# Gathering graph rows on one Trainium2 core: fifteen or twenty-three chunks fetched row by row, by one queue or by two

## What is computed

```
xn   = layernorm(x)
agg  = segment_sum(xn[src], dst)            # 106250 edges, sorted by dst
h    = relu(agg @ W_rel + b_rel + xn @ W_root)
c    = sigmoid(i) * tanh(g);  y = (sigmoid(o) * tanh(c)) @ W_fc + b_fc     # i, g, o = h @ W_ih.T + b
x2   = x + y
w    = softmax over slices of layernorm(x2) @ W_x @ W_slice ...
out  = x2 + attention over slice tokens, spread back by w
```

## Time and profile before

| | us |
|---|---|
| median of 3 runs | 1237.53 (1236.96 to 1239.23) |
| profiled execution | 1240.34 |
| its span of instructions | 1238.5 |
| TensorE busy in the span | 1116.1 |
| ScalarE busy | 627.2 |
| GpSimd busy | 805.3 |

### The profile page before, as it was taken

The page is one execution under the profiler, slowest core; times in us unless marked ns, Lnnn a source line. Parts: engine busy times, 40 slices in busy tenths (PEclk is TensorE's granted clock), DMA queues, the critical chain, the costliest instruction groups (busy, mean ns, idle before and its releaser), DMA issues. The chain is left out here.

```text
span 1238.5 us, 30254 instructions
## 1 busy us (share of the span) xinstructions
PE 1116.1 (90%) x9821; PEld 967.1 (78%) x9821; DVE 831.8 (67%) x2560; ACT 627.2 (51%) x1257; POOL 805.3 (65%) x856
## 2 busy tenths in 40 slices
PE   1077799999999999999999999999999999999998
PEld 0046688878888888788888787888888878897798
DVE  7885476667666766676677756775767566746665
ACT  5872444554456454545554545455545454555332
POOL 5877777777777777777777777777777777400000
PEclk9998999999999999999999999999999999999999
DMA  8674444444454445444544444444444454313498
GB/s 313 225 268 119 125 130 136 147 142 136 129 148 142 141 124 150 140 140 123 150 149 138 121 148 150 137 121 150 147 136 122 150 149 137 97 44 116 129 336 290
DMA packets 92966, 188.74 MB, mean 152 GB/s; under 512 B 20914, under 2 KB 55591, under 8 KB 92821
## 3 DMA queue, kind: packets, MB, share of 16 engines
q0 software_dynamic: 39168, 107.01, 30.0%
q1 hardware_dynamic: 42794, 59.89, 14.8%
q10 hardware_dynamic: 10859, 20.05, 4.5%
HBM read 154.87 MB, written 32.00 MB: 151 GB/s over the span
## 5 line engine op out<-in xcount | busy, mean ns | idle before, releaser
L700 POOL DMA_INDIRECT ring<-table,sidx x798 | 763.5, 957 | 247.5 <-issue 242.7
L419 PE MATMUL ps<-h_h,wih_h 128*128 128x250 f32 x1200 | 338.8, 282 | 0.0
L420 PE MATMUL ps<-h_l,wih_h 128*128 128x250 f32 x1200 | 336.5, 280 | 0.0
L421 PE MATMUL ps<-h_h,wih_l 128*128 128x250 f32 x1200 | 336.5, 280 | 0.0
L419 PEld LDWEIGHTS ps<-h_h,wih_h 128*128 128x128 f32 x1200 | 230.1, 192 | 2.0 <-issue 0.8
L420 PEld LDWEIGHTS ps<-h_l,wih_h 128*128 128x128 f32 x1200 | 230.2, 192 | 1.1
L421 PEld LDWEIGHTS ps<-h_h,wih_l 128*128 128x128 f32 x1200 | 230.1, 192 | 0.0
L850 ACT ACTIVATE gate<-ps,bgate 128x250 f32<-128x250 f32 x300 | 124.2, 467 | 140.7 <-PE ps L421 139.7
L651 DVE TENSOR_SCALAR oneh<-iota,didx 128x64 f16<-128x64 f16 (+2 forms) x1179 | 183.1, 259 | 0.0
L1078 PE MATMUL ps<-ring,oneh 128*32 128x512 f16 x2280 | 151.0, 391 | 34.5 <-DMA ring<-table,sidx 31.9
L1078 PEld LDWEIGHTS ps<-ring,oneh 128*32 128x32 f16 x2280 | 59.5, 97 | 107.7 <-DMA ring<-table,sidx 46.4
(11 more groups left out here) (213 smaller groups left out, 2508.4 us busy)
## 6 DMA issues: line engine op xcount, KB each, us to landing
sp_ring<-table SPq DMA_DIRECT2D x1920, 1.0 KB
ring<-table,sidx POOLq DMA_INDIRECT x798
swt_d<-swt ACTq DMA_DIRECT2D x25, 500.0 KB
gate<-swt_d SPq DMA_DIRECT2D x19, 500.0 KB, 5.9
x_room<-in_x SPq DMA_DIRECT2D x12, 512.0 KB, 10.6
xn<-table SPq DMA_DIRECT2D x25, 224.0 KB
xin<-in_x SPq DMA_DIRECT2D x25, 224.0 KB
res<-xin SPq DMA_DIRECT2D x25, 224.0 KB
```

Of the source, the lines that this page charges most:

```text
L419: eng.matmul(dst, wh, xh, start=first, stop=False)
L420: eng.matmul(dst, wh, xl, start=False, stop=False)
L421: return eng.matmul(dst, wl, xh, start=False, stop=last)
L700: pool.indirect_dma_start(ring[:, j, :], None, table, bass.IndirectOffsetOnAxis(ap=idx, axis=0)).then_inc(done, 16)
```

## The change

Twenty-three chunks in place of fifteen are fetched row by row: chunk 86 and every 33rd after it, so about one in each turn. Of each chunk's 128 rows, SyncE fetches the first 88 and ScalarE the last 40, both into the same ring of three chunks and with the same semaphore. SyncE fetches 8, 16 and 64 rows in its turn's three places, and 88 in turn 0; it loads 22 addresses at a time. ScalarE fetches 20 rows in turn 0 and then rows at eleven places in its turn; it loads addresses 10 at a time at four of these. Both wait for room in the ring at a chunk's first row (`wait_slot`). ScalarE's turns are written out one by one, without a loop. The helpers for the slot, the addresses and one row are moved out of SyncE's block so that both can use them.

```diff
-    SP_FIRST, SP_STEP, SP_N, SP_SLOTS = 86, 52, 15, 3
+    SP_FIRST, SP_STEP, SP_N, SP_SLOTS = 86, 33, 23, 3
-    ROWS_FIRST, ROWS, LOADS = 96, (8, 16, 60), 32
+    ROWS_FIRST, ROWS, LOADS = 88, (8, 16, 64), 22
+    SP_ROWS = 4 * LOADS
+    ACT_ROWS = P - SP_ROWS
+    ACT_FIRST, ACT_LOADS = 20, 10
+        def wait_slot(eng, k):
+            if k == 0:
+                eng.wait_ge(spi_done, 1)
+            if k >= SP_SLOTS:
+                b = last_reader(SP_CHUNKS[k - SP_SLOTS])
+                eng.wait_ge(sum_done[b % 2], b // 2 + 1)
+                eng.wait_ge(sum_done[(b - 1) % 2], (b - 1) // 2 + 1)
+        def fetch_row(eng, k, q, start):
+            to = sp_ring[q:q + 1, k % SP_SLOTS, :].bitcast(U8)
+            eng.dma_start(to, rows8[ds(start, row_bytes)].rearrange("(p c) -> p c", p=1)).then_inc(
+                sp_rows[k % SP_SLOTS], 16)
...
+            def load_rows():
+
+                r = loaded[0]
+                if r < last_row and r < row_at[0] + ACT_LOADS:
+                    k, q = r // ACT_ROWS, r % ACT_ROWS
+                    if q == 0:
+                        wait_slot(act, k)
+                    for i, start in enumerate(load_starts(act, k, SP_ROWS + q, ACT_LOADS)):
+                        starts[r + i] = start
+                    loaded[0] += ACT_LOADS
+            def fetch_rows(n):
+
+                for r in range(row_at[0], min(row_at[0] + n, loaded[0])):
+                    fetch_row(act, r // ACT_ROWS, SP_ROWS + r % ACT_ROWS, starts.pop(r))
+                    row_at[0] += 1
...
                 if gnn:
                     split_x(t - 1)
+                    load_rows()
+                    fetch_rows(9)
                     relu_h(t - 1, 0)
...
-                    gates(t - 1, 0, 4)
+                    fetch_rows(2)
+                    gates(t - 1, 0, 2)
+                    load_rows()
+                    fetch_rows(1)
+                    gates(t - 1, 2, 4)
                     tanh_c(t - 1, 0)
+                    load_rows()
+                    fetch_rows(9)
...
-                    gates(t - 1, 4, 8)
+                    gates(t - 1, 4, 6)
+                    fetch_rows(1)
+                    gates(t - 1, 6, 8)
                     tanh_c(t - 1, 1)
+                    fetch_rows(4)
                     gates(t - 1, 8, 10)
+                    load_rows()
+                    fetch_rows(3)
...
                     gates(t - 1, 10, 12)
+                    fetch_rows(1)
                     high_hl(t - 1, 0)
+                    fetch_rows(1)
                     tanh_c(t - 1, 3)
...
                 if gnn:
+                    fetch_rows(1)
                     high_hl(t - 1, 1)
...
                     act.dma_start(swt_d[ds(p, 1)].rearrange("a p n -> p (a n)"),
                                   swt[:, :, :, :].rearrange("p e j n -> p (e j n)")).then_inc(swt_st, 16)
+                    fetch_rows(9)
...
-            with act.Fori(lo, hi, step) as t:
+            for t in range(lo, hi, step):
                 two_turns(turn, t)
```

More of the change, by code:

```diff
@@ L438, in out_count, with load_starts @@
             return 16 * (len(range(q, NCH + 1, TILES)) + (len(REST_PARTS) - 1 if q == NCH % TILES else 0))
+        rows8 = table.bitcast(U8).rearrange("n c -> (n c)")
+        row_bytes = 4 * C
+        def wait_slot(eng, k):
[5 more added lines that the diff above has]
+                eng.wait_ge(sum_done[(b - 1) % 2], (b - 1) // 2 + 1)
+        def load_starts(eng, k, q, n):
+            _, at = nc.values_load_multi_w_load_instructions(
+                sp_idx[k:k + 1, q:q + n], engines=[eng.engine], min_val=0, max_val=(N - 1) * row_bytes,
+                skip_runtime_bounds_check_because="the DMA checks its bounds")
+            return at
+        def fetch_row(eng, k, q, start):
+            to = sp_ring[q:q + 1, k % SP_SLOTS, :].bitcast(U8)
+            eng.dma_start(to, rows8[ds(start, row_bytes)].rearrange("(p c) -> p c", p=1)).then_inc(
+                sp_rows[k % SP_SLOTS], 16)
         @block.sync
@@ L517, in _ @@
             row_at = [0]
-            rows8 = table.bitcast(U8).rearrange("n c -> (n c)")
-            row_bytes = 4 * C
             def fetch_rows(n):
-                for r in range(row_at[0], min(row_at[0] + n, SP_N * P)):
-                    k, q = r // P, r % P
+                for r in range(row_at[0], min(row_at[0] + n, SP_N * SP_ROWS)):
+                    k, q = r // SP_ROWS, r % SP_ROWS
                     if q == 0:
[L526 to L531, removed]
-                    if q % LOADS == 0:
[L533 to L539, removed]
+                        wait_slot(sp, k)
+                    if q % LOADS == 0:
+                        starts[:] = load_starts(sp, k, q, LOADS)
+                    fetch_row(sp, k, q, starts[q % LOADS])
                 row_at[0] += n
@@ L548, in turn @@
                     for j, k in SP_OF.items():
-                        assert first_reader(j) // 2 > t or row_at[0] >= (k + 1) * P, (t, j, k, row_at)
+                        assert first_reader(j) // 2 > t or row_at[0] >= (k + 1) * SP_ROWS, (t, j, k, row_at)
                 if gather:
@@ L579, in _ @@
             last_turns(turn)
-            assert row_at[0] >= SP_N * P
+            assert row_at[0] >= SP_N * SP_ROWS
             def f_load(n, k):
@@ L873, in copy_out @@
                                ACT.Copy).then_inc(att_a, 1)
-            def turn(t, odd, gather, gnn, ffn, ahead):
+            row_at, loaded, starts = [0], [0], {}
+            last_row = SP_N * ACT_ROWS
+            def load_rows():
[11 more added lines that the diff above has]
+                    row_at[0] += 1
+            def turn(t, odd, gather, gnn, ffn, ahead):
+                if gather and t < NP - 1:
+                    for j, k in SP_OF.items():
+                        assert first_reader(j) // 2 > t or row_at[0] >= (k + 1) * ACT_ROWS, (t, j, k, row_at)
+                if t == 0:
+                    for _ in range(ACT_FIRST // ACT_LOADS):
+                        load_rows()
+                        fetch_rows(ACT_LOADS)
                 if gnn:
                     split_x(t - 1)
+                    load_rows()
+                    fetch_rows(9)
                     relu_h(t - 1, 0)
@@ L936, in _ @@
             lo, hi, step = turns(turn)
-            with act.Fori(lo, hi, step) as t:
+            for t in range(lo, hi, step):
                 two_turns(turn, t)
             last_turns(turn)
+            assert row_at[0] == last_row
             def f_high(n, k):
```

## The result

The median goes from 1237.37 us (four runs, the three of the first table among them) to **1343.74 us** (1337.74 to 1345.85), a ratio of 1.0849 with a 95% interval of 1.0821 to 1.0876. The forecast was 1228.2 us in a range of 1226 to 1241: wrong in sign and far outside the range. The profiled execution took 1343.31 us around a span of 1341.5, 103.0 more than before.

A forecast was written before the change was run, and what follows sets the result against it. GpSimd's gather issue was taken as the bound: 10.1 us saved gives 849.1 us for 21 turns, TensorE with ScalarE's delay 849.7; so -9.3 us from 1237.53, 1228.2 us, range 1226 to 1241.

The forecast's parts named there:

- the price of SyncE's loads: SyncE's address loads: 0.053 us a further word, 1.60 us for 22; four a turn (6.4 us) replace 2.6 of 32, +0.8 us.
- The sentence behind it: SyncE's queue: without slack it would fall behind by tenths of a microsecond a turn, harmless as its loads are needed later.
- The slack: SyncE's wait for TensorE's transposes, 3.4 us a turn: at least 0.8 us is left, so SyncE's added work costs nothing.
- SyncE without any wait: Sign on SyncE's queue, listed among those that would show a step of the forecast wrong; no size given.
- A turn without waits of 39.96 us: TensorE's loop turn without any wait for gathered rows: 39.96 us, the median of seven, against 40.91 on average.
- What GpSimd is spared: GpSimd's gathers in the loop: 790 instead of 798 at 1.262 us each, 10.1 us less; GpSimd stays the bound.
- the no-gain rival: GpSimd's gathers: the added row transfers slow each by 13 ns, taking the 10.1 us; 1237.5 us, chance 0.12.
- The pitch of ScalarE's rows: ScalarE's queue: 0.32 us a row as on SyncE, bounds 0.26 and 0.41; issues don't wait for the running activation.
- The last batch outruns its cover: Slower rival, ScalarE's nine rows behind swt's store: at 0.41 us a row the graph layer is late; 1244.8 us, chance 0.16.
- ScalarE's loads: ScalarE's queue: four loads of 10 addresses a turn at 0.97 us each, standing in waits and costing nothing.
- the partial-gain rival: ScalarE's rows slower or begun after split_x's copies: relu_h and the norm late, 0.8 us a turn; 1234.3 us, chance 0.16.

## Why the prediction was wrong

**The step that failed is the price of SyncE's loads**: "0.053 us a further word and, as an estimate, 1.60 us for 22". It drew a line through two rows, one word and 32 words, of which the loads of 32 all begin on a multiple of 16 bytes. The 22 words lay between the two in length but not in kind: half of the new loads start at words 22 and 66. I had forecast 6.4 us of loads a turn of SyncE; they took 13.52. The term was +0.8 us a turn against the loads of before, and measured +7.9 (13.52 - 5.66, the loads of before over the same turns). For aligned starts the estimate was near: 22 words take 1.84 us, and the aligned loads 6.34 a turn.

**The sentence behind it was right at its size and not beyond.** The slack, "at least 0.8 us", is 1.45 us in the version with the rows moved. That falling behind "by tenths of a microsecond a turn" costs nothing holds: with one load doubled SyncE has no wait left and the time is unchanged. But I looked only at the rows that SyncE would deliver late. In the kernel before, the start of SyncE's turn (its load of xn) lies 20.7 us behind the start of TensorE's in turn 1, and only 1.1 us behind from turn 3 on. With the change it is 24.8 us in turn 1 and still 20.5 in turn 3; at 5 us a turn it is 29.3 in turn 5. With that the lead is used up: turn 5 (265.18 to 311.60 us) is the first of 46 us. (With one load doubled it is at most 8.4 us from turn 3 on, so nothing is lost.) From there SyncE sets the pace, and what comes late first is not a row but the load of x, in order on the same queue. No rival had SyncE as its place; "SyncE without any wait" stood only in the list of what would show a step wrong, without a price. A load of 22 words, seen nowhere before, had been given one estimate and no upper bound, so the range was too narrow, too.

**What stood in no term at all** is TensorE's clock behind a wait: of the 103.0 us, 68.3 are TensorE idle and 34.7 its longer busy time. A turn without waits of 39.96 us was reckoned at the full clock.

**What GpSimd is spared** was right in size: forecast -10.1 us, measured -10.6 in the version where neither queue stands in the way; the gathers kept their time, 956 ns against 957. With that the no-gain rival falls. That this version's 1228.0 us are also the forecast's 1228.2 bears out this term alone: the forecast had nine rows behind the store, and with nine there it is 1235.8. I gave the no-gain rival 0.12 partly for a rule of the Trainium skill ("DMA: Bandwidth & Descriptors", "Why a DMA increments its semaphore by 16 and not by 1"): a copy without an outer dimension to divide, as of one row, runs on one engine. The pages of the two profiles fit that: 12699 packets on ScalarE's queue (q10) against 10859 before, two more for each of its 920 rows, one of 1 KB and one of 4 bytes. No row here tells on which engine the rows ran, but whatever that engine carries, it doesn't slow the gathers.

**The pitch of ScalarE's rows** was right: 235 ns an issue, ten rows in 3.16 us in the version with the rows moved, and they are issued beside activations, as the earlier trace rows let expect. ScalarE there, in order of time:

```profile
505.27 0.59 ACT L822 ACTIVATE at_h<-ps 128x500 fp32r<-128x500 f32 x1 [1.72 <-PE ps L1154]
505.35 0.57 ACTq L463 DMA_DIRECT2D sp_ring<-table  x2
...
506.66 3.16 ACTq L463 DMA_DIRECT2D sp_ring<-table  x10
```

**The last batch outruns its cover**: right in mechanism and place, too small in size. Nine rows were to take 2.9 us; behind the store they take 3.1 to 3.7, because one issue, mostly the third, takes 0.4 to 0.95 us in each of the 21 turns, which stood in no term. I had 0.5 us a turn, on 39.96; nine rows there with aligned loads give 40.89, so 0.93, just short of the 0.95 at which the gain is gone: 1235.8 us, 0.2% below before.

**ScalarE's loads** were mis-sized like SyncE's (0.97 us forecast, 2.39 for every second one), which is the partial-gain rival's mechanism, relu_h and the norm behind it late, by way of the loads instead of the rows. In the change as made it is hidden behind SyncE. With SyncE's loads aligned it has the larger part in the 35 us between 1266.2 and 1230.9: nine rows behind the store with aligned loads, the other batches moved, take 1235.8, so the ninth row has some 5 us in them, as an estimate.

So the change holds a gain that the starts of its loads undo: with 24 and 20 words for 22, and 12 and 8 for 10, it is 1230.9 us, and with ScalarE's rows moved from behind the store, too, 1228.0, the whole 10 us.

## What to carry to other kernels

A cost between two measured sizes is bounded by the rows only if nothing but the size differs; here the start address did, and a queue that runs in order charged the difference to everything behind it. For a queue with little slack, work out its whole turn (here 39.12 us of work in 40.54) and put the worst price of each new instruction into that sum before calling it hidden. When a queue does fall behind, look for the first thing on it that another engine waits for, not for the thing that was added.

## What the runs showed of the hardware

- A load of n words from SBUF into registers takes, on top of some 0.3 us, 0.22 us for four words from a start at a multiple of 16 bytes, and 0.20 to 0.21 us for each single word from any other start: 22 words 1.84 or 4.69 us, 32 words 2.08 or 6.70.
- Behind the issue of the 500 KB store on ScalarE's queue, one of the next row issues takes 0.4 to 0.95 us, mostly about 0.7, instead of 0.235. SyncE's long issues fall there too: of its 2024 row issues 22 took over 400 ns, 19 of these within 3 us of a store. Why was not tested.
- In 18 of the 21 turns of the changed kernel TensorE stood idle for 2.3 to 7.7 us before the transposes; its granted clock fell to 0.50, its 1.2 GHz level, in that time or up to 1.9 us behind it, and stayed there for some microseconds (588.67 to 595.50 in the turn above). Before, with waits of up to 1.6 us, the records of these turns show no fall.
